# An fp32 attention block with split fp16 products: the softmax is transposed by DMA instead of TensorE, and the steps of the loop are shifted against each other

## The reference

```
h = layernorm(x)                                  # x: 8 x 128 x 512
q = (h @ Wq)                                      # 32 heads of 128
k, v = concat([ctx, h]) @ Wk, ... @ Wv            # 256 keys per batch, 4 heads of 128
p = softmax(q k^T / sqrt(128))                    # for each batch and head 128 x 256
x = x + (p v) @ Wo
x = x + ffn(layernorm(x))                         # weights quantised in blocks of 32
```

## Time and profile before

| | |
|---|---|
| median of 3 runs | 944.35 us (943.86 to 945.84) |
| the profiled execution: span, first to last instruction | 944.5 us |
| PE, DVE, ACT, POOL busy | 91%, 70%, 48%, 27% |
| loads and weights, before the first exponential | to 104.9 us |
| attention, to the start of its last `project` | 104.9 to 693.0 us |
| feed-forward stage | about 700 us to the end |

### The profile page before, as it was taken

The page is one execution under the profiler, slowest core; times in us unless marked ns, Lnnn a source line. Parts: engine busy times, 40 slices in busy tenths (PEclk is TensorE's granted clock), DMA queues, the critical chain, the costliest instruction groups (busy, mean ns, idle before and its releaser), DMA issues. The chain is left out here.

```text
span 944.5 us, 16272 instructions
## 1 busy us (share of the span) xinstructions
PE 861.5 (91%) x5390; PEld 539.1 (57%) x5390; DVE 663.7 (70%) x1333; ACT 452.6 (48%) x1029; POOL 256.4 (27%) x382
## 2 busy tenths in 40 slices
PE   9999999999899999989999999999868999900898
PEld 3444777767577776657766677767533444400343
DVE  5754588886478888558888656667647459989741
ACT  5344455645346554436554454454513029868630
POOL 0000245453235464224455322222210002203000
PEclk9999999999989999999999999999998999965799
DMA  8013022222012313002232620000030000000001
GB/s 289 1 56 111 20 84 90 90 68 90 3 57 80 111 45 112 23 25 77 92 101 75 210 74 1 2 1 1 1 123 1 1 0 1 1 0 0 12 33 45
DMA packets 39756, 52.14 MB, mean 55 GB/s; under 512 B 2432, under 2 KB 18816, under 8 KB 39680
## 3 DMA queue, kind: packets, MB, share of 16 engines
q1 hardware_dynamic: 39680, 51.13, 16.7%
HBM read 40.37 MB, written 10.75 MB: 54 GB/s over the span
## 5 line engine op out<-in xcount | busy, mean ns | idle before, releaser
L523 ACT ACTIVATE arena<-bank 128x512 f16<-128x512 f32 (+1 forms) x329 | 189.5, 599 | 342.8 <-PE bank L363 234.9
L698 DVE SCALAR_TENSOR_TENSOR arena<-bank,arena 128x512 f16<-128x512 f32 (+1 forms) x329 | 219.1, 686 | 87.8 <-ACT arena L523 87.7
L270 PE MATMUL bank<-arena 128*128 128x256 f16 (+2 forms) x1872 | 261.8, 292 | 0.0
L270 PEld LDWEIGHTS bank<-arena 128*128 128x128 f16 (+1 forms) x1872 | 183.8, 98 | 69.0
L1067 POOL TENSOR_SCALAR arena<-arena,rsum 128x256 f32<-128x256 f32 x256 | 135.2, 528 | 241.2 <-DVE rsum L792 223.5
L465 PE MATMUL bank<-arena 128*128 128x512 f16 x528 | 116.3, 384 | 8.9 <-DVE arena L698 8.9
L387 PE MATMUL bank<-arena 128*128 (+1 forms) x512 | 121.0, 379 | 0.7 <-ACT arena L523 0.7
L579 ACT ACTIVATE arena<-bank,nmax 128x256 f32<-128x256 f32 x256 | 118.1, 487 | 6.2 <-DVE nmax L788 6.2
L784 DVE TENSOR_REDUCE nraw<-bank 128x2 f32<-128x512 f32 x128 | 85.4, 689 | 36.1 <-PE bank L352 36.1
L352 PE MATMUL bank<-arena 128*128 (+1 forms) x768 | 97.4, 277 | 9.4 <-issue 7.2
L352 PEld LDWEIGHTS bank<-arena 128*128 128x128 f16 x768 | 75.8, 99 | 33.6 <-issue 11.2
(11 more groups left out here) (91 smaller groups left out, 738.9 us busy)
## 6 DMA issues: line engine op xcount, KB each, us to landing
arena<-in_w_units SPq DMA_DIRECT2D x33, 256.0 KB, 2.8
w_ready<-arena SPq DMA_DIRECT2D x33, 256.0 KB, 2.1
arena<-w_ready SPq DMA_DIRECT2D x3, 2816.0 KB, 10.9
arena<-in_wq SPq DMA_DIRECT2D x32, 256.0 KB, 2.9
arena<-in_wo SPq DMA_DIRECT2D x32, 256.0 KB, 2.7
arena<-in_x SPq DMA_DIRECT2D x1, 2048.0 KB, 15.4
out<-arena SPq DMA_DIRECT2D x8, 256.0 KB, 2.0
arena<-in_wk SPq DMA_DIRECT2D x4, 256.0 KB, 5.2
```

The source lines that it names most:

```text
L270: last = nc.tensor.matmul(bank, a(i, c), b(j, c), start=start and c == 0 and n == 0, stop=stop and c == chunks - 1 and n == 2)
L523: return nc.scalar.activation(dst, src, ACT.Copy, scale=scale)
L698: return nc.vector.scalar_tensor_tensor(out=dst, in0=src, scalar=scale, in1=part, op0=ALU.mult, op1=ALU.subtract)
```

## The change

- The eight PE transposes and their PSUM banks go. p is split before it is turned: `p_upper` on ACT makes the fp16 upper part of the normalised p (128 x 1024, SBUF to SBUF), `p_lower` on DVE the lower part, and `turn_p` on SP turns both with one DMA (128 x 2048 fp16 in, 16 blocks of 128x128 out). The instructions on ACT and DVE that split the transposed p (two each) go.
- The freed banks hold a second set of scores: `scores`, `maxima`, the exponentials, `reciprocals` and `normalise` run two steps ahead (`AHEAD`), with p, its sums and their reciprocals in two buffers. `maxima` becomes one reduction over 1024 columns and one small instruction.
- q is projected six steps ahead instead of four (`Q_AHEAD`), so its weights for the next group are loaded and split in steps 5 to 10 instead of 7 to 12. `project` runs one step behind.
- `add_y` moves from odd steps to the even step after. `wo_part` on ACT moves ahead of the upper part of the head output, `unit_lo` on DVE ahead of `maxima`.
- In group 3 the feed-forward weights come in 22 loads between the turns instead of two large ones, and some addresses in SBUF move.

```diff
-LATE = 12
+AHEAD = 2
+Q_AHEAD = 6
+LATE = QUADS - Q_AHEAD
...
+            def turn_p(t, k):
+                sp.wait_ge(p_lo, t + 1)
+                sp.sem_inc(sp_passed, 1)
+                sp.dma_start_transpose(pt_s[:, k % 2].rearrange("p r c (h t) -> p (r c h) t", h=4),
+                                       p_16[:, k % 2].rearrange("p r n -> p (r n)")).then_inc(pt_loaded[k % 2], 16)
+
+            turn_p(0, 0)
             with sp.Fori(0, NG - 1) as g:
                 load_unit(g, 0)
                 for k in range(QUADS):
                     if k < GH:
                         load_wo(g + 1, k)
-                    if k == 7:
+                    if k == 5:
                         load_wq(g + 1, 0)
                         load_wq(g + 1, 1)
-                    if 9 <= k <= 11:
-                        load_wq(g + 1, 2 * (k - 8))
-                        load_wq(g + 1, 2 * (k - 8) + 1)
+                    if 7 <= k <= 9:
+                        load_wq(g + 1, 2 * (k - 6))
+                        load_wq(g + 1, 2 * (k - 6) + 1)
+                    turn_p(g * QUADS + k + 1, k + 1)
                     if 1 <= k <= FT:
                         store_unit(g, k - 1)
                     if k < FT - 1:
                         load_unit(g, k + 1)
...
             def step(g, k):      # PE
-                scores(*((g, k + 1) if k < QUADS - 1 else (g + 1, 0)))
-                transpose_p(g, k)
+                scores(*((g, k + AHEAD) if k < QUADS - AHEAD else (g + 1, k + AHEAD - QUADS)))
                 if not last(g) and 1 <= k <= FT:
                     transpose_w(g, k - 1)
+                if k >= 1:
+                    project(g, k - 1)
...
+            def p_upper(t, k):   # ACT
+                act.wait_ge(norm_out, t + 1)
+                hi(p_16[:, k % 2, 0, :], p_s[:, k % 2].rearrange("p c h t -> p (c h t)"), 1.0).then_inc(p_hi, 1)
...
+            def p_lower(t, k):   # DVE
+                dve.wait_ge(p_hi, t + 1)
+                lo(p_16[:, k % 2, 1, :], p_s[:, k % 2].rearrange("p c h t -> p (c h t)"), p_16[:, k % 2, 0, :], 1.0).then_inc(p_lo, 1)
...
             def step(g, k):      # DVE
                 if not (final and k == QUADS - 1):
-                    maxima(t + 1)
-                for c in range(2):
-                    dve.wait_ge(pt_hi, 2 * t + c + 1)
-                    lo(pt_s[:, 1, c, :], banks[TR + c][:, :], pt_s[:, 0, c, :], 1.0).then_inc(tr_free, 1)
+                    p_lower(t + 1, k + 1)
+                if not final and 1 <= k <= FT:
+                    unit_lo(g, k - 1)
+                if not (final and k >= QUADS - AHEAD):
+                    maxima(t + AHEAD, k + AHEAD)
                 if not final and k < FT:
                     unit_scales(g, k)
-                if not (final and k == QUADS - 1):
-                    reciprocals(t + 1)
-                if not final and 1 <= k <= FT:
-                    unit_lo(g, k - 1)
...
+                if not (final and k >= QUADS - AHEAD):
+                    reciprocals(t + AHEAD, k + AHEAD)
...
             def step(g, k):      # POOL
-                if not (final and k == QUADS - 1):
-                    normalise(t + 1)
+                if not (final and k >= QUADS - AHEAD):
+                    normalise(t + AHEAD, k + AHEAD)
```

More of the change, by code:

```diff
@@ L353, in scores, with head_out @@
                                                   kv5[:, g + 1, r, :, b * P:(b + 1) * P], start=n == 0, stop=n == 2)
[L354 to L359, removed]
+                mm.then_inc(sc_mm, 1)
+            def head_out(g, k):
+                b = k // 2
+                pe.wait_ge(pt_loaded[k % 2], 16 * (g * (QUADS // 2) + k // 2 + 1))
                 for c in range(2):
[L361 to L368, removed]
-                for c in range(2):
-                    pe.wait_ge(tr_free, 2 * t + c + 3)
                     for n, (i, r) in enumerate(((0, 0), (0, 1), (1, 0))):
                         mm = nc.tensor.matmul(banks[OB][:, :], kv[:, g + 1, 2 + i, (c * B + b) * P:(c * B + b + 1) * P],
-                                              pt_s[:, r, c, :], start=c == 0 and n == 0, stop=c == 1 and n == 2)
+                                              pt_s[:, k % 2, r, c, :], start=c == 0 and n == 0, stop=c == 1 and n == 2)
                 mm.then_inc(pv_mm, 1)
@@ L589, in step @@
                 t = g * QUADS + k
-                final, late = last(g), last(g) and k >= LATE
-                for c in range(2):
-                    act.wait_ge(tr_mm, 2 * t + c + 1)
-                    hi(pt_s[:, 0, c, :], banks[TR + c][:, :], 1.0).then_inc(pt_hi, 1)
+                final, late, q = last(g), last(g) and k >= LATE, k + Q_AHEAD
                 if not (final and k == QUADS - 1):
-                    exps(t + 1)
-                if late:
-                    for b in X2_AT[k]:
-                        copy_x2(b)
+                    p_upper(t + 1, k + 1)
                 if not final and 1 <= k <= FT:
                     unit_hi(g, k - 1)
+                if not (final and k >= QUADS - AHEAD):
+                    exps(t + AHEAD, k + AHEAD)
+                if late:
+                    for b in X2_AT.get(k, ()):
+                        copy_x2(b)
+                if not final and 1 <= k <= GH:
+                    wo_part(g + 1, k - 1)
                 act.wait_ge(pv_mm, t + 1)
@@ L604, in step @@
                 if not late:
-                    q_part(t + 4, (k // 4 + 1) % 2, 2 * (k % 4), QB)
-                if not final and 1 <= k <= GH:
-                    wo_part(g + 1, k - 1)
+                    q_part(t + Q_AHEAD, (q // 4) % 2, 2 * (q % 4), QB)
             def copy_x2(b):
@@ L612, in copy_x2 @@
                                      ACT.Copy, scale=1.0).then_inc(x2_copied, 1)
-            for f in range(4):
+            for f in range(Q_AHEAD):
                 if f == 3:
-                    exps(0)
-                q_part(f, 0, 2 * f, QB + f % 2)
+                    exps(0, 0, first=True)
+                if f == 5:
+                    exps(1, 1, first=True)
+                    p_upper(0, 0)
+                q_part(f, f // 4, 2 * (f % 4), QB + f % 2)
             with act.Fori(0, NG - 1) as g:
@@ L884, in step @@
                     ln2_apply(k // 2 - 1)
-                if k % 2 and not late:
+                if k == QUADS - 1:
                     add_y(k // 2, t)
-            for f in range(4):
+            for f in range(Q_AHEAD):
                 if f == 3:
-                    maxima(0)
-                    reciprocals(0)
-                q_part(f, 0, 2 * f, QB + f % 2)
+                    maxima(0, 0)
+                    reciprocals(0, 0)
+                if f == 5:
+                    maxima(1, 1)
+                    reciprocals(1, 1)
+                    p_lower(0, 0)
+                q_part(f, f // 4, 2 * (f % 4), QB + f % 2)
             with dve.Fori(0, NG - 1) as g:
@@ L1112, in _ @@
             pool.sem_inc(w_dq, 1)
-            normalise(0)
+            normalise(0, 0)
+            normalise(1, 1)
             with pool.Fori(0, NG - 1) as g:
```

144 lines of the change are left out of this document (78 added, 66 removed).

## The result

The changed kernel takes 1010.06 us (median of 4 runs, 1006.74 to 1011.1), the kernel before 944.75 (4 runs): ratio 1.0686, 95% interval 1.0653 to 1.0719. The forecast was 973 us with a range of 935 to 1,004. It had the direction; the time lies 37 us above it and 6 us above its range.

The account below looks back on a forecast made before the run. PE bound the kernel before; afterwards rings of waits through other engines and SP's queue would. Groups of 156.2 us, jumps, group 3, start and end put the last `project` at 722 against 693.0: 973 us, range 935 to 1,004.

Parts of the forecast that it names:

- ring B: Every step: waits from `reciprocals` through `normalise`, `p_upper`, `p_lower`, `maxima` and exponentials to the next `reciprocals`, 8.3 us.
- rings A and C: Steps 1 to 6: waits through DVE and ACT (A, 9.2 us) and through `transpose_w` and `project` (C, 9.3); 9.3 taken.
- SP's queue: Steps 7 to 9: turn and raw-unit load stand behind waiting Wq loads; unit arrives 7.4 us in.
- the late steps: Steps 8 to 10 of a group, lengthened by the late raw unit: 13.7 us and twice 12.7.
- Step 0: First step of a group, taken as paced by ring B alone: 8.3 us.
- TensorE's clock: Named sign of certain failure: PE, idle an eighth of the time, is granted a lower clock.
- the end of group 3: After the last `reciprocals`: `normalise` 2.5, `p_upper` 1.1, `p_lower` 1.3, turn 4, `head_out` 1.3, upper part 0.7 us.
- PE's saving: Transposes of p leave PE: 0.88 us a step, leaving 7.81, or 8.24 with a weight unit.
- the jumps: The two jumps back: 1.5 us charged for each, the interval near 10 us instead of 14.
- Group 3: Odd steps 8.3 us; even ones 9.7, where the second layer norm holds DVE.
- the queue hides: Rival: the rings hold, but the raw unit's lateness on SP's queue hides: 942 to 957 us, chance 0.18.
- the turn paces everything: Rival: the transposing DMA outlasts a step and is the bound: 1,130 us at 12 us each, chance 0.08.

Follow-up runs that it names:

- experiment 1: Changed kernel with SP issuing the turn, store and raw unit's load ahead of the two Wq loads in steps 7 to 9: 972.82 us.
- experiment 2: Changed kernel with only the turn moved ahead of the two Wq loads in steps 7 to 9: 993.39 us.
- experiment 3: Changed kernel with a plain DMA of the same bytes in place of the transposing one, p not turned: 994.04 us.
- experiment 4: Changed kernel with `p_lower` and `unit_lo` behind `maxima` on VectorE: 980.04 us.
- experiment 5: Changed kernel with the edits of experiment 1 and experiment 4 together: 948.29 us.
- experiment 6: Experiment 5 plus `transpose_w` behind `project` on PE: 900.39 us.
- experiment 7: Experiment 5 plus `unit_lo` behind `reciprocals`, `unit_hi` behind the exponentials and `wo_part` at the step's end, their old places: 939.92 us.
- experiment 8: Experiment 7 plus `transpose_w` behind `project` on PE, all edits together: 895.92 us.
- experiment 9: Changed kernel with `transpose_w` behind `project` as the only edit: 1006.05 us.
- experiment 11: Changed kernel; in steps 8 to 10 `unit_scales` behind `reciprocals` on VectorE and `normalise` ahead of `unit_normalise` on GpSimd: 996.68 us.

## Where the prediction was right, and which of its terms failed

The paths were right: ring B, rings A and C and SP's queue are where the time went, and the edits that shorten them gave it back (experiments 1 to 8). The sum failed in its sizes. The largest part is the late steps: forecast 13.7 and twice 12.7 us in each group, measured 12.8 to 15.7, 15 us more over three groups. Step 0, ring A's terms, TensorE's clock and the end of group 3 are the rest.

**PE's saving.** Right: 0.88 us a step, 7.81 and 8.24 to 8.25 where PE is the bound (experiments 4 and 8). None of it shortened the changed kernel, since PE was not the bound in any step outside the jumps.

**Ring B.** Right in path and size: 8.27 against 8.3, undone by one move (experiment 4). The terms bounded from other shapes held: `p_lower` a mean of 1.24 us (1.22; its working, 951 ns and 256 columns at the pace of 1,207 for 1024, gives 1.25), `p_upper` 1.06. `normalise` started 0.38 after `reciprocals`, as said.

**Group 3, the start and the end.** Group 3 was right: 9.8 and 8.3 in turn (eight steps of 8.3 and six of 9.7 are 124.6, not 124.8). Of the start's 1.3 us for the first raw unit, the trace shows a wait of 0.3, and `reciprocals` of 2 came at 122.66 (forecast 123.0). From the last `reciprocals` to the last `project` I had 10.9 us; it took 15.0 (741.52 to 756.55). The last `head_out` stands behind a `project` and, ahead of that, transposes of the second layer norm's output, which waited 1.87 us for VectorE. The sum left that path out.

**Rings A and C in steps 1 to 6.** Right that both lie above PE and near each other (experiments 4, 6, 7, 9), mis-sized: 9.3 taken, 9.7 measured. The changed kernel's VectorE shows the terms:

```profile
344.80 0.67 DVE L721 SCALAR_TENSOR_TENSOR arena<-bank,arena 128x512 f16<-128x512 f32 x1
345.39 2.30 DVE L721 SCALAR_TENSOR_TENSOR arena<-arena 128x512 f32 x2
347.61 0.68 DVE L721 SCALAR_TENSOR_TENSOR arena<-bank,arena 128x512 f16<-128x512 f32 x1
348.21 1.21 DVE L806 TENSOR_REDUCE nraw<-bank 128x4 f32<-128x1024 f32 x1
...
352.69 0.69 DVE L721 SCALAR_TENSOR_TENSOR arena<-bank,arena 128x512 f16<-128x512 f32 x1 [0.83 <-ACT arena L536]
353.30 0.65 DVE L835 TENSOR_SCALAR arena<-arena 128x512 f32<-128x512 f32 x1
353.98 0.58 DVE L837 TENSOR_SCALAR arena<-arena 128x512 f32<-128x512 f32 x1
354.48 0.67 DVE L721 SCALAR_TENSOR_TENSOR arena<-bank,arena 128x512 f16<-128x512 f32 x1
```

Wo's part and `p_lower` cost 347.61 - 345.39 = 2.22 where I had 0.85 + 1.14 = 1.99; `unit_round` 354.48 - 353.30 = 1.18, not 0.96. These two are nearly all of the difference. Both read and write SBUF and ran beside POOL, `unit_round` beside `normalise` (352.07 to 354.28). But the row that gave me 0.96 also ran beside `normalise` (341.27 to 343.69 in the kernel before), so why they cost more here is open.

**Step 0.** I had only ring B in it, 8.3; it took 9.7, 9.9 and 9.4, 4 us over three groups. In the interval that starts there the next step's `unit_lo` already stands ahead of `maxima`, and it waits for the first unit: in group 0 `transpose_w` waited 2.66 us for POOL's dequantising.

**SP's queue.** The wait was right: `unit_scales` waited 37.8 us in all, and the forecast's 7.4 - 3.2 in nine steps is the same. What failed is what a late unit costs. "+2.8 in step 8, +3.3 in 9 and 10" made 28 us in all, and the queue's order is worth 37 (experiment 1). I had followed the late unit only on VectorE. Behind it on POOL stand `unit_normalise`, `normalise` and the dequantising, and the next step's `p_lower` and `unit_lo` wait for their end; the moves that take `normalise` out of that row gave 13 us (experiment 11). "I take 4, and a hold of 2, midway": the landing was 4.4 and the median hold 2.02, but behind the Wq loads, where it counts, the hold was 2.7 to 3.6; why it is longer there was not tried.

**Steps 9 and 10 without the queue.** "Steps 9 and 10, without Wo: 9.4" were 10.1 to 11.5 with the queue in order (experiment 1), 8 us over three groups. In the first of the two in group 1 a pair of Wq's lower parts and `p_lower` took 3.42 us (372.40 to 375.82) instead of 2.74. The rest is partly the clock.

**TensorE's clock.** "Wrong for certain if [...] PE, now idle an eighth of the time, is granted a lower clock": it was, and the sum had nothing for it. Experiment 1's timeline of PE, then a stretch of it with busy times, granted clock, DMA:

```profile
374.27 0.66 PE L408 MATMUL bank<-ident,arena 128*128 128x128 f32 x4 [3.14 <-POOL arena L1115]
374.76 3.44 PE L395 MATMUL bank<-arena 128*128 x8
378.00 1.20 PE L399 MATMUL bank<-arena 128*128 x4
...
375.00:378.00 3.00, 3.00 (x9) 1.03 (x8) 2.96 (x5) 0.67 (x2) 0.62 (x1) 0.50 0.83 216
```

After a wait of 3.14 us for POOL `project` ran at half clock and took 4.28 us to its successor instead of 2.59; `head_out` came later by that, and VectorE waited 2.40 us for its upper part (382.47). This happened five times in groups 0 to 2 of experiment 1, always behind the wait of `transpose_w`. The five intervals are 0.7 to 1.4 us longer than the same steps of the groups where it did not happen, some 6 us together. No run keeps the clock up with the waits as they are, so that is an estimate. The changed kernel has five such places too.

**The jumps.** Right in kind: 10.5 and 11.3 instead of 14; 9.8 was forecast.

**Rivals.** That the queue hides was wrong by 37 us. That the turn paces everything was wrong: 4.4 us, and a plain copy in its place changes no ordinary step. The Trainium skill's 1,309 ns for a 128x128 transpose by DMA ("VectorE: DVE Perf Modes", the three transpose paths) does not add up block by block here: 16 blocks in one DMA landed in 4.4 us. By the Trainium skill's "Advanced Engine Details and Errata" (X-Bar Transpose), such a DMA is about as fast as an ordinary one; the trace agrees roughly: 4.4 against 3.2 us.

In sum, of the 37 us that were missing, experiment 1 divides: about 9 belong to the queue (37 instead of 28), and 28 are there without it (973, where I had 945). Of the 28, steps 0 to 6 make some 15 (4 in step 0, 3 the clock, 8 ring A's terms), steps 9 and 10 8 (about half of it the clock), the jumps 2, the end of group 3 another 3, steps 7 and 8 together 1, and the median's distance from the profiled span 1. Steps 11 to 14 were 2 shorter than forecast.

## What to carry to other kernels

When work leaves the engine that is the bound, draw the rings of waits through the others before counting the gain: here a bound of 7.8 us met three rings of 8.3 to 9.7, and the order inside one engine's step (`p_lower` ahead of `maxima`, `transpose_w` ahead of `project`) was what closed them. Rings of equal length hide each other, so that the edit which gives 48 us behind two others gives 4 alone. Here PE was also granted a lower clock behind some of its waits, and its work there grew too. A load that was ready to go, but stands behind a wait in a DMA queue, costs on every engine that handles its data in order; put the entries whose waits end last at the end of a queue's step.

## What the runs showed of the hardware

- Four `normalise` instructions took 2.15 us on POOL while VectorE mostly worked from PSUM or was idle, and 3.28 while it ran SBUF to SBUF instructions. `p_lower` on VectorE took 1.40 at 382.00, where it began beside POOL's dequantising, and 1.23 where POOL was idle. What is shown is that they go together.
- A transposing DMA of 512 KB inside SBUF landed in 4.4 us (4.2 to 6.2) and held SP's queue for 2.0 us (1.4 to 3.6); a plain one 3.2 and 0.47.
- PE's granted clock fell to half, its lower level of 1.2 GHz, in places after waits of 2.2 to 5.8 us, but not behind each (after 2.66 us at 126.95 it stayed full). The changed kernel in two stretches (busy times, then granted clock): behind its wait of 4.15 us for POOL at 396.73 it ran at half, and `project`'s first eight matmuls took 3.62 us, not 1.89.

```profile
360.00:370.00 10.00, 8.37 (x59) 5.55 (x58) 8.20 (x14) 5.01 (x13) 4.09 (x6) 1.00 0.16 47
...
397.00:402.00 5.00, 5.00 (x15) 2.18 (x15) 2.89 (x4) 1.88 (x7) 1.24 (x2) 0.50 1.06 220
```
